# Small-format feed-forward stages: the product of the rounded h with its block scales is issued on VectorE instead of GpSimd

## What is computed

```python
def fp4_quant_dequant(x):                      # blocks of 16 along the last dim
    xb = x.reshape(shape[:-1] + (shape[-1] // BLOCK, BLOCK))
    scale = jnp.max(jnp.abs(xb), axis=-1, keepdims=True) / 6.0
    scale = jnp.maximum(scale, jnp.float32(1e-12))
    xn = xb / scale
    idx = jnp.searchsorted(_MID, jnp.abs(xn))
    q = _GRID[idx] * jnp.sign(xn) * scale
    return q.reshape(shape)
def fp4_linear(x, w):
    return jnp.einsum('bsk,nk->bsn', fp4_quant_dequant(x), fp4_quant_dequant(w))
gate = fp4_linear(x, w_gate)                   # x: layernorm of the residual, 256 wide
y = fp4_linear(x, w_up)                        # 704 wide
h = jax.nn.silu(gate) * y
return fp4_linear(h, w_down)                   # h is quantised too, in 44 blocks of 16 per token
```

## Time and profile before

| | us |
|---|---|
| median of 3 runs | 2261.66 |
| lowest, highest | 2257.74, 2266.56 |
| the profiled execution, its own time | 2277.73 |
| its span, first to last instruction | 2275.9 |
| PE busy, DVE busy over the span | 1893.5, 1707.0 |

### The profile page before, as it was taken

How to read it: one execution, slowest core, us unless ns; L and a number is a source line. 1 busy time by engine, 2 the same in 40 slices (tenths; PEclk the granted TensorE clock), 3 DMA queues, 4 the chain that set the end, 5 groups by cost and what they waited for, 6 DMA issues and landing times. The chain is left out here.

```text
span 2275.9 us, 37061 instructions
## 1 busy us (share of the span) xinstructions
PE 1893.5 (83%) x11875; PEld 1340.2 (59%) x11875; DVE 1707.0 (75%) x3526; ACT 1007.7 (44%) x1972; POOL 799.4 (35%) x862
## 2 busy tenths in 40 slices
PE   2799997799997369889797799999999874588898
PEld 1677787687775257778674233333333362477787
DVE  8789874688886666768887777777777366676688
ACT  1333435333334523335565355555555635233345
POOL 2223321233333667773346000000000036677733
PEclk9999997999998669999998799999999986699999
DMA  5000001000002512234347254353342016122246
GB/s 181 1 1 0 0 1 35 22 1 0 0 1 77 184 47 86 87 89 146 105 117 173 39 71 56 51 71 56 51 71 37 1 56 206 40 87 89 87 138 194
DMA packets 116656, 156.61 MB, mean 69 GB/s; under 512 B 20967, under 2 KB 85773, under 8 KB 115981
## 3 DMA queue, kind: packets, MB, share of 16 engines
q1 hardware_dynamic: 99840, 112.83, 21.4%
q0 software_dynamic: 14400, 40.41, 5.7%
q10 hardware_dynamic: 2252, 1.29, 0.2%
HBM read 107.00 MB, written 47.20 MB: 68 GB/s over the span
## 5 line engine op out<-in xcount | busy, mean ns | idle before, releaser
L2083 DVE TENSOR_REDUCE t_nm<-ps 128x1 f32<-128x512 f32 (+3 forms) x768 | 390.5, 552 | 102.3 <-PE ps L2173 50.7
L2149 ACT ACTIVATE t_E<-ps 128x1024 f32<-128x1024 f32 (+3 forms) x384 | 295.1, 808 | 244.4 <-PE ps L2201 191.1
L1569 PE MATMUL ps<-m_w,m_xT 128*128 (+1 forms) x1248 | 347.9, 414 | 10.3 <-DVE m_xT L1649 9.0
L1569 PEld LDWEIGHTS ps<-m_w,m_xT 128*128 128x128 f32 x1248 | 223.2, 192 | 53.2 <-issue 14.9
L693 PE MATMUL ps<-wdT,f_hT 128*128 128x256 f32 (+1 forms) x768 | 194.8, 396 | 18.2 <-ACT f_hT L735 18.2
L2198 PE MATMUL ps<-t_Qs,t_Ks 98*128 98x512 bf16 (+3 forms) x768 | 198.6, 339 | 5.0 <-DMA t_Qs<-t_mT 3.9
L1587 PE MATMUL ps<-m_w,m_hT 128*128 (+1 forms) x1248 | 201.5, 297 | 0.5 <-DVE m_hT L1666 0.5
L1656 DVE TENSOR_TENSOR m_ab<-ps,m_b 128x512 f32<-128x512 f32 x208 | 142.4, 685 | 68.5 <-PE ps L1569 45.2
L2068 POOL COPY t_Va<-t_V 128x128 f32<-128x128 f32 x64 | 16.1, 295 | 487.0 <-DVE t_mp L2094 486.8
L192 POOL TENSOR_TENSOR f_h<-f_h,f_hs 128x704 f32<-128x704 f32 x64 | 88.7, 1386 | 276.2 <-DVE f_h L230 276.2
L1621 ACT ACTIVATE m_hT<-ps 128x256 fp32r<-128x256 f32 x208 | 79.9, 384 | 223.5 <-PE ps L1578 135.2
(11 more groups left out here) (299 smaller groups left out, 3975.4 us busy)
## 6 DMA issues: line engine op xcount, KB each, us to landing
m_raw<-in_L_ffn_rw SPq DMA_DIRECT2D x48, 256.0 KB, 3.2
t_parts<-t_qkv_part SPq DMA_DIRECT2D x64, 192.0 KB, 2.8
t_Qs<-t_parts SPq DMA_DIRECT2D x96, 128.0 KB, 4.1
t_Ks<-t_parts SPq DMA_DIRECT2D x96, 128.0 KB, 6.7
m_yl<-m_picked_out SPq DMA_DIRECT2D x40, 256.0 KB, 2.9
m_rows<-m_xn SPq DMA_DIRECT2D x16, 512.0 KB, 4.2
m_xg<-m_rows SPq DMA_DIRECT2D x64, 128.0 KB
m_y<-m_picked_out SPq DMA_DIRECT2D x24, 256.0 KB, 3.1
```

Source lines behind the costliest of these rows:

```text
L1569: last = nc.tensor.matmul(ps[:, H1 + u, :], xT[:, u, kx, k, :], of_expert(w1, kw, e, k), start=n == 0, stop=n == 3 * DC - 1)
L2083: nc.vector.tensor_reduce(dst, ps[:, bank, 0:n], AX_X, ALU.max, negate=True).then_inc(emptied, 1)
L2149: nc.scalar.activation(E[:, s % NPB, :, 0:n], ps[:, bank:bank + 2, 0:n], ACT.Exp, scale=float(HD) ** -0.5).then_inc(e_ok, 1)
```

## The change

The product of the rounded h with its block scales is taken out of POOL's list (`h_finish` with its wait on `h_round`, once before the steps and once in each step but the last) and put into DVE's `snap_h`, behind a drain. The semaphore `h_round` is gone, and `h_quant`, for which PE waits, is now raised by DVE. 32 products in each of the two stages are concerned.

```diff
             def snap_h(n, buf):
 
                 dve.wait_ge(h_grid, n + 1)
-                fp4_snap(nc, h[:, buf, :], hmagic[:, buf % 2, :]).then_inc(h_round, 1)
+                fp4_snap(nc, h[:, buf, :], hmagic[:, buf % 2, :])
+                nc.vector.drain()
+                fp4_times(nc.vector, h[:, buf, :], HB, hs[:, buf, 1, :]).then_inc(h_quant, 1)
...
-            def h_finish(n, buf):
-
-                pool.wait_ge(h_round, n + 1)
-                fp4_times(nc.gpsimd, h[:, buf, :], HB, hs[:, buf, 1, :]).then_inc(h_quant, 1)
-
             rows.rstd(pool, 1)
             rows.divide(pool, 1)
-            h_finish(0, 0)
             rows.rescale(pool, 1)
 
             def step(n, g, s, end):
                 j = s % GT
-                if exists(n, 1):
-                    h_finish(n + 1, (s + 1) % 4)
```

More of the change, by code:

```diff
@@ L531, in fp4_ffn @@
         x_turned, x_high, x_split = sem("x_turned"), sem("x_high"), sem("x_split")
-        gate_ok, up_ok, silu_ok, h_ok, h_div, h_grid, h_round, h_quant = map(
-            sem, ("gate", "up", "silu", "h", "h_div", "h_grid", "h_round", "h_quant"))
+        gate_ok, up_ok, silu_ok, h_ok, h_div, h_grid, h_quant = map(
+            sem, ("gate", "up", "silu", "h", "h_div", "h_grid", "h_quant"))
         h_turned, h_stored, down_ok, x_added = map(sem, ("h_turned", "h_stored", "down", "x_added"))
```

## The result

| | before | after |
|---|---|---|
| median, us | 2262.87 (4 runs) | 2311.26 (4 runs) |
| lowest, highest | 2257.74, 2266.56 | 2307.09, 2323.54 |
| the profiled execution | 2277.73 | 2307.35 |
| ratio of the runs, 95% interval | | 1.0229, 1.02 to 1.0259 |

The account below looks back on a forecast made before the run. DVE was taken to bound the rounds. Per stage 1.39 + 23.3 - 0.7 + 1.73 = 25.7 us, 51.5 us for both, added to the 2261.66 us median: 2313 us, 2.3% slower, range for 8 in 10 2303 to 2325.

Parts of the forecast that it names:

- The bound: In the rounds DVE is the bound, with PE, POOL and ACT following; a round takes 34.50 us, PE's work 31.85.
- The price: Each product moved to DVE adds 0.89 us plus 0.08 us drain, 0.97 us; 24 in a stage's rounds, +23.3 us.
- Ahead of the steps: Tile 0: POOL's product of x holds the new DVE product, today's L181 stall goes; net +1.39 us a stage.
- The tail: Tiles 25 to 31: +2.21 us at tile 28, three steps give back 0.16 each, 1.73 us left a stage.
- the sum: One stage: 1.39 + 23.3 - 0.7 + 1.73 = 25.7 us longer.
- The size, 51.5 against 48 us: Both stages together were to cost 51.5 us, 25.7 us each, the other stages only starting later.
- The clock of TensorE: In the rounds PE busy 83% of 38.3 us, granted clock 1.00, pauses of some 1.6 us in every step.
- rival 2: TensorE's granted clock falls towards 1.2 GHz in the rounds, a round up to 51 us; 2325 to 2480 us; 4%.
- Rivals 1 and 3: First: PE's chain decides the rounds, at best 2258 us, 3%; third: POOL's stalls of DVE vanish, -33 us, 2281 us, 3%.
- Rival 1: Not slower: PE's chain, not DVE's, decides the rounds; at best 4 us gained in all, 2258 us; 3%.
- Rival 4: The tail hides nothing, or the new product meets POOL more often: 64 x 0.97 = 62 us, 2324 us; 5%.

## Why the prediction was right, and where it was off

- **The bound.** That VectorE decides in the rounds rested on it having no wait but one inside its own chain, while its busy share was lower than PE's. The run without a product and the run with two confirm it from both sides: 0, 1 and 2 products on VectorE give rounds of 34.40, 38.26 and 42.12 us, twice 3.86 us for four products, 0.965 each.
- **The price.** 0.89 us and 0.08 us of drain, worked out from two rows of the same line at other sizes, were 0.89 and 0.08 in the rounds.
- **Ahead of the steps.** +1.39 us was said for tile 0, with the product held by GpSimd's product of x. From the timeline of VectorE in after:

```profile
77.41 2.46 DVE L192 TENSOR_TENSOR f_h<-f_h,f_hs 128x704 f32<-128x704 f32 x1
...
80.76 0.89 DVE L179 TENSOR_REDUCE f_hs<-f_h 128x44 f32<-128x704 f32 x1
81.72 0.19 DVE L181 TENSOR_SCALAR f_hs<-f_hs 128x44 f32<-128x44 f32 x1
81.99 0.43 DVE L183 RECIPROCAL f_hs<-f_hs 128x44 f32<-128x44 f32 x1
```

  The first product took 2.46 us, L181 behind it 0.19 instead of 1.33, and L183 came at 81.99. It came at 79.85 before, and the stage began 0.74 us later: +1.40 us.
- **The tail.** At the last L565 of the stage 331.04 became 357.08; less the 0.74 us, that is +25.3 us where the sum had 25.7. The steps of the tail gave back what was said: one wait of 0.15 us for PE is left of the three of 1.13. Of the missing 0.4 us, 0.3 are a gap in the first round of before, 0.41 us ahead of L183 where 0.07 is usual, which stage f0 of after doesn't have. The profile shows no cause for it. In f1 both kernels have such a gap, and the sum came to +25.5 us.
- **The size, 51.5 against 48 us.** The runs can't tell these two apart: the interval of 45 to 59 us holds both. The 47.5 us of the two profiled stages fell short for a reason that the sum took as it stood, the down product of tile 30 at the stage end. It runs at the lower clock in one execution and at the full one in another, 1.7 us for each stage, and by chance the two profiles fell on different sides. With equal clock the stages cost 25.3 to 25.5 us each, where 25.7 was predicted.
- **The clock of TensorE.** Here the prediction was wrong. I expected PE to be busy for 83% of a round, a granted clock of 1.00, and pauses of 1.6 us in every step, in front of L677 (L671 in after). None of them came, and a clock under 1.00 in the rounds had been named as a sign of being wrong. The longest waits of PE in the rounds of after (98 to 327 us) and the granted clock of two stretches in them:

```profile
PE ps L640 <- POOL f_xn L192: 14.0, 6, 2.4
...
PE ps L651 <- DVE f_h L565: 6.4, 6, 1.1
...
PE ps L651 <- DVE f_xT L558: 5.2, 6, 1.8
```

```profile
98.00:327.00 229.00, 196.74 (x1051) 165.45 (x1050) 206.14 (x318) 78.14 (x161) 32.89 (x30) 0.97 0.00 0
...
126.00:136.00 10.00, 10.00 (x51) 8.57 (x50) 8.86 (x13) 2.83 (x6) 0.00 (x0) 0.83 0.01 2
```

  From the timeline of PE in after, the same place in two rounds:

```profile
125.75 0.69 PE L640 MATMUL ps<-ident,f_xn 128*128 128x128 f32 x4 [2.31 <-POOL f_xn L192]
126.24 4.64 PE L687 MATMUL ps<-wdT,f_hT 128*128 128x256 f32 x12
...
202.27 0.66 PE L640 MATMUL ps<-ident,f_xn 128*128 128x128 f32 x4 [2.31 <-POOL f_xn L192]
202.76 2.95 PE L687 MATMUL ps<-wdT,f_hT 128*128 128x256 f32 x12
```

  PE's idle time gathers in front of the turn of x, 2.3 us in one piece once a round, where it waits for GpSimd's product of x. Behind that pause the down product took 4.01 to 4.64 us instead of 2.95 in 8 of the 12 rounds of both stages, and in the first round shown the clock was 0.83 over 10 us. With that PE was busy for 32.9 us a round, 86%. The rounds were 38.26 us all the same, slow down product or not. So rival 2 began to happen, and cost nothing, for the reason given: PE has 38.3 us for 32.9 us of work.
- **Rivals 1 and 3** ended with the run without a product. Rival 1 rested on the rule of the Trainium skill (GPSIMD Engine Reference, 4.1 Engine selection) that elementwise work belongs on VectorE. The durations here agree in direction (1.39 against 0.89 us, a factor 1.56, where the section says about 2), and following the rule cost 48 us, since it compares engines and not lists.
- **Rival 4** had the tail at full price. The tail took up most of one product (+1.7 us there where six products would cost 5.8), and of the second next to nothing. Its 62 us lie just over the interval of 45 to 59 us.

## What to carry to other kernels

The slower engine can be the right one: here an operation was nearly free at 1.4 us on the engine whose time is hidden, and cost 0.97 us on the engine that has no wait outside its own chain. Look for the engine that waits for nobody, not for the busiest, and before moving work onto it ask for its idle time in each stage. The stall beside GpSimd's product was met with work that isn't held by it (here the statistics), and then with a look at who was fed by the moved work, since about half of the gain was lost at ACT until rstd was moved along.

## What the runs showed of the hardware

- While GpSimd multiplies in SBUF, a VectorE operation with two SBUF inputs stands still to the end of it (2.51 for 0.89 us, in both stages of every kernel; the new product took 2.46 us in the same way), and so does a tensor_scalar of 128x44 (0.90 for 0.19). The statistics (1.40 us) and L565, which reads PSUM (0.88), don't. Which property of the tensor_scalar makes it wait was not tried apart. It holds the other way round too: GpSimd's product of x took 2.38 and 2.51 us instead of 1.94 where it started while VectorE was in L230 or L228 (in after at 76.75 and 85.90 us).
- After a pause of 1.7 to 1.8 us at the stage end, PE's next 12 matmuls took 4.7 us in some executions and 3.05 in others; after 2.3 to 2.4 us in the rounds of after, 4.01 to 4.64 us in eight rounds and 2.95 in four. What decides it is open.
